# Selective scan of a Mamba block: two states in one scan instruction, the products with C in place over the states

## The reference, cut to what matters

```python
dt = jax.nn.softplus(dt_r @ W_dt + b_dt)
A = -jnp.exp(A_log)
h = 0                                             # [batch, 512 channels, 16 states]
for t in range(512):                              # lax.scan over the tokens
    dA = jnp.exp(dt[t][..., None] * A)            # "decay"
    h = dA * h + dt[t][..., None] * B[t][:, None, :] * x[t][..., None]     # the last term: "drive"
    y[t] = jnp.einsum('bds,bs->bd', h, C[t])
y = y + xc * D
y = y * jax.nn.silu(z)
attn = y @ W_out
P = x @ U1;  H = gelu(P @ V1 + b1);  Q = H @ U2;  ffn = Q @ V2 + b2        # beside it, used as a gate
```

## Time and profile before

| | us |
|---|---|
| time, median of 3 runs | 4176.64 (4173.5 to 4176.8) |
| span of the profiled execution | 4176.4 |
| scan stage in it, from the first drive to the last store | 304 to 1181, 877 long |
| busy in the stage: DVE / POOL / PE / ACT | 832.7 / 790.8 / 761.2 / 573.1 |

### The profile page before, as it was taken

How to read it: one execution, slowest core, us unless ns; L and a number is a source line. 1 busy time by engine, 2 the same in 40 slices (tenths; PEclk the granted TensorE clock), 3 DMA queues, 4 the chain that set the end, 5 groups by cost and what they waited for, 6 DMA issues and landing times. The chain is left out here.

```text
span 4176.4 us, 58564 instructions
## 1 busy us (share of the span) xinstructions
PE 3436.1 (82%) x17002; PEld 1831.7 (44%) x17002; DVE 3225.2 (77%) x5162; ACT 2286.7 (55%) x2729; POOL 1675.2 (40%) x783
## 2 busy tenths in 40 slices
PE   6847898889979978759799995699986977787775
PEld 3412333333347756635344442599975541222112
DVE  6869999999978877637687785487775768888884
ACT  4756666666622335424366663122212648989995
POOL 0008998989931100022000000000024338889986
PEclk9878999999989989968799998899998987888887
DMA  3453333333223357538423231211113452334332
GB/s 105 162 194 138 126 129 117 130 128 132 96 81 117 120 135 180 131 101 275 109 72 75 65 80 34 91 43 48 40 56 113 146 155 89 120 109 122 118 111 66
DMA packets 294113, 465.41 MB, mean 111 GB/s; under 512 B 40439, under 2 KB 237688, under 8 KB 273518
## 3 DMA queue, kind: packets, MB, share of 16 engines
q1 hardware_dynamic: 243590, 406.11, 30.0%
q10 hardware_dynamic: 50408, 57.97, 5.2%
HBM read 322.44 MB, written 141.33 MB: 111 GB/s over the span
## 5 line engine op out<-in xcount | busy, mean ns | idle before, releaser
L3314 POOL TENSOR_TENSOR distance_dist<-distance_dist,distance_least_all 128x2048 f32<-128x2048 f32 x128 | 577.0, 4537 | 113.5 <-DMA distance_least_all<-distance_least_rows 101.5
L1044 PE MATMUL mamba_psum<-mamba_hc,mamba_ident 128*128 128x512 f32 x1024 | 544.8, 643 | 86.7 <-DVE mamba_hc L947 69.9
L886 POOL TENSOR_TENSOR mamba_drive<-mamba_u,mamba_b_all 128x1024 f32<-128x1024 f32 x256 | 597.7, 2352 | 21.6 <-DMA mamba_b_all<-bc 21.6
L934 ACT ACTIVATE mamba_psum<-mamba_dt,mamba_a_neg 128x512 f32<-128x512 f32 x512 | 334.6, 683 | 288.7 <-DVE mamba_hc L947 281.6
L969 DVE TENSOR_TENSOR_SCAN mamba_psum<-mamba_psum,mamba_drive 128x512 f32<-128x512 f32 x352 | 414.9, 1215 | 43.7 <-POOL mamba_drive L886 29.4
L2355 DVE TENSOR_REDUCE causal_row_max<-causal_psum 128x1 f32<-128x512 f32 x512 | 332.7, 683 | 113.1 <-PE causal_psum L2411 103.0
L1044 PEld LDWEIGHTS mamba_psum<-mamba_hc,mamba_ident 128*128 128x128 f32 x1024 | 176.3, 195 | 410.6 <-DVE mamba_hc L947 223.5
L2314 ACT ACTIVATE causal_probs<-causal_psum 128x1024 f32<-128x1024 f32 x256 | 252.4, 1022 | 118.2 <-PE causal_psum L2434 116.0
L3407 DVE TENSOR_REDUCE distance_least<-distance_psum 128x2 f32<-128x1024 f32 x256 | 294.5, 1214 | 14.6 <-PE distance_psum L3466 14.1
L3425 DVE TENSOR_SCALAR distance_dist<-distance_psum 128x1024 f32<-128x1024 f32 x192 | 227.1, 1220 | 99.4 <-PE distance_psum L3481 93.4
L3466 PE MATMUL distance_psum<-distance_shared_k_stacks,distance_shared_q_stacks 102*128 102x512 bf16 x512 | 206.2, 499 | 118.1 <-DVE distance_least L3407 56.4
(11 more groups left out here) (455 smaller groups left out, 8228.5 us busy)
## 6 DMA issues: line engine op xcount, KB each, us to landing
mamba_b_all<-bc SPq DMA_DIRECT2D x32, 1024.0 KB
mamba_c_all<-bc SPq DMA_DIRECT2D x32, 1024.0 KB, 6.6
distance_least_all<-distance_least_rows SPq DMA_DIRECT2D x32, 1024.0 KB, 4.6
expert_weights_w<-L_ffn_w SPq DMA_DIRECT2D x16, 1024.0 KB, 4.8
z<-mamba_in_z SPq DMA_DIRECT2D x8, 1024.0 KB
xc<-mamba_in_xc SPq DMA_DIRECT2D x8, 1024.0 KB, 3.9
dt<-mamba_in_dt SPq DMA_DIRECT2D x8, 1024.0 KB, 3.9
u<-mamba_in_u SPq DMA_DIRECT2D x8, 1024.0 KB, 4.2
```

The lines of the kernel that those rows point to most:

```text
L886: pool.tensor_tensor(drive[:, n % DRIVES:n % DRIVES + 2], u[:, slot, m].unsqueeze(1).broadcast_to([P, 2, T]), b_all[:, s:s + 2], ALU.mult) ...
L934: act.activation(ps[:, DECAY_BANK + n % RING], dt[:, slot, m], ACT.Exp, scale=a_neg[:, m, s:s + 1]).then_inc(decay_ready, 1)
L1044: pe.matmul(ps[:, Y_BANK + m % 2], ident[:, :], hc[:, n % PRODUCTS], start=False, stop=(s == DS - 1)).then_inc(y_summed, 1)
L3314: pool.tensor_tensor(dist[:, g % 2, kt], dist[:, g % 2, kt], least_all[:, g % 2], ALU.subtract).then_inc(shifted, 1)
```

## The change

Two states (a pair `p`) are scanned in one instruction over 1024 elements. The decays of a pair lie in two neighbouring PSUM banks, of which two pairs exist; the decay of token 0 is never written by ACT and stays 0.0 from a memset at the stage's start, so that the state does not run over from the first state's last token into the second's first. The scan always writes to SBUF, `h`, a ring of 4 pairs. The products with C are made in place over `h`, on DVE for 11 of 16 states (`ON_DVE`: per 8 pairs, three instructions of one state and four of two) and on POOL for 5 (`ON_POOL`: three of one state and one of two). The drives are made four states at a time, in a ring of two such chunks. `hc` is gone. ACT's exponentials of pair p wait for the scan of pair p-2; the scan of pair p waits until PE has summed pair p-4.

```diff
-RING = 4
+PAIRS = STEPS // 2
 CHUNK = 4
-DRIVES, PRODUCTS = 8, 8
-POOL_STATES = (2, 5, 8, 11, 14)
+DRIVES, STATES = 2, 4
+ON_POOL = {0: slice(0, 1), 2: slice(0, 1), 4: slice(0, 1), 6: slice(0, 2)}
+ON_DVE = {0: slice(1, 2), 1: slice(0, 2), 2: slice(1, 2), 3: slice(0, 2), 4: slice(1, 2), 5: slice(0, 2), 7: slice(0, 2)}
...
-        drive = c.sb("drive", [P, DRIVES, T])
-        h = c.sb("h", [P, 2, T])
-        hc = c.sb("hc", [P, PRODUCTS, T])
+        drive = c.sb("drive", [P, DRIVES, CHUNK, T])
+        h = c.sb("h", [P, STATES, 2, T])
...
+        def decays(p):
+            return ps[:, DECAY_BANK + p % 2 * 2:DECAY_BANK + p % 2 * 2 + 2]
+        def state(p, part):
+            return h[:, p % STATES, part]
+        def c_rows(p, part):
+            first = p * 2 % DS
+            return c_all[:, first + part.start:first + part.stop]
...
 GpSimd
+                def times_c(p, b):
+                    part = ON_POOL[p % (DS // 2)]
+                    pool.wait_ge(h_ready, b * PAIRS + p + 1)
+                    if p < DS // 2:
+                        pool.wait_ge(c_loaded[p * 2 // CHUNK], b * DMA + DMA)
+                    pool.tensor_tensor(state(p, part), state(p, part), c_rows(p, part), ALU.mult).then_inc(hc_pool_ready, 1)
...
                 def scan(n, b, slot):
+                    if n % CHUNK:
+                        return
-                    if n % 2 == 0:
-                        wait_past(pool, h_ready, b * STEPS + n + 2 - DRIVES)
-                        pool.tensor_tensor(drive[:, n % DRIVES:n % DRIVES + 2], u[:, slot, m].unsqueeze(1).broadcast_to([P, 2, T]),
-                                           b_all[:, s:s + 2], ALU.mult).then_inc(drive_ready, 1)
-                    if n >= 3 and on_pool(n - 3):
-                        times_c(n - 3, b)
+                    wait_past(pool, h_ready, b * PAIRS + (n + CHUNK - DRIVES * CHUNK) // 2)
+                    pool.tensor_tensor(drive[:, n // CHUNK % DRIVES], u[:, slot, m].unsqueeze(1).broadcast_to([P, CHUNK, T]),
+                                       b_all[:, s:s + CHUNK], ALU.mult).then_inc(drive_ready, 1)
+                    if n:
+                        times_c((n - CHUNK) // 2, b)
+                    if n == STEPS - CHUNK:
+                        times_c(n // 2, b)
...
 ScalarE
+                act.wait_ge(starts_made, 1)
...
-                    if n >= RING:
-                        if on_pool(n - RING):
-                            act.wait_ge(h_ready, b * STEPS + n - RING + 1)
-                        else:
-                            act.wait_ge(hc_ready, b * DVE_HC + dve_products(n - RING))
...
-                    act.activation(ps[:, DECAY_BANK + n % RING], dt[:, slot, m], ACT.Exp, scale=a_neg[:, m, s:s + 1]).then_inc(decay_ready, 1)
+                    if not second:
+                        wait_past(act, h_ready, b * PAIRS + p - 1)
+                    act.activation(decays(p)[:, second, 1:], dt[:, slot, m, 1:], ACT.Exp,
+                                   scale=a_neg[:, m, s:s + 1]).then_inc(decay_ready, 1)
...
 VectorE
+                dve.memset(ps[:, DECAY_BANK:DECAY_BANK + 4, 0:1], 0.0).then_inc(starts_made, 1)
+                dve.wait_ge(starts_made, 1)
...
-                    dve.tensor_tensor(hc[:, n % PRODUCTS], ps[:, DECAY_BANK + n % RING], c_all[:, n % DS], ALU.mult).then_inc(hc_ready, 1)
+                    dve.tensor_tensor(state(p, part), state(p, part), c_rows(p, part), ALU.mult).then_inc(hc_ready, 1)
...
-                    if m >= 1 and s == 5:
+                    if m >= 1 and s == 6:
                         gated(b, slot, m - 1)
-                    dve.wait_ge(decay_ready, b * STEPS + n + 1)
...
-                    dve.tensor_tensor_scan(out, bank, drive[:, n % DRIVES], 0.0, ALU.mult, ALU.add).then_inc(h_ready, 1)
-                    if n >= 1 and not on_pool(n - 1):
-                        times_c(n - 1, b)
+                    dve.wait_ge(decay_ready, b * STEPS + n + 2)
+                    dve.wait_ge(drive_ready, b * NCHUNK * MT + n // CHUNK + 1)
+                    wait_past(dve, y_summed, b * STEPS + n + 2 - 2 * STATES)
+                    flat = "p s t -> p (s t)"
+                    dve.tensor_tensor_scan(state(p, slice(0, 2)).rearrange(flat), decays(p).rearrange(flat),
+                                           drive[:, n // CHUNK % DRIVES, n % CHUNK:n % CHUNK + 2].rearrange(flat),
+                                           0.0, ALU.mult, ALU.add).then_inc(h_ready, 1)
+                    if p >= 1 and (p - 1) % (DS // 2) in ON_DVE:
+                        times_c(p - 1, b)
+                    if p == PAIRS - 1:
+                        times_c(p, b)
...
 TensorE
-                    pe.matmul(ps[:, Y_BANK + m % 2], ident[:, :], hc[:, n % PRODUCTS], start=False, stop=(s == DS - 1)).then_inc(y_summed, 1)
+                    if n % 2:
+                        return
+                    p = n // 2
+                    for table, ready, count in ((ON_DVE, hc_ready, DVE_HC), (ON_POOL, hc_pool_ready, POOL_HC)):
+                        part = table.get(p % (DS // 2), slice(0, 0))
+                        for k in range(part.start, part.stop):
+                            if k == part.start:
+                                pe.wait_ge(ready, b * count + products(table, p))
+                            pe.matmul(ps[:, Y_BANK + m % 2], ident[:, :], h[:, p % STATES, k], start=False,
+                                      stop=(s + k == DS - 1)).then_inc(y_summed, 1)
```

More of the change, by code:

```diff
@@ L734, in nothing, with products @@
     pass
[L737 to L750, removed]
+def products(table, p):
+    m, pair = divmod(p, DS // 2)
+    return m * len(table) + sum(k <= pair for k in table)
 def stage_mamba_scan(nc, w, x_in, xc_in, z_in, dt_in, u_in, bc_in, low_in, x_out):
@@ L881, in scan @@
                         pool.wait_ge(du_loaded[slot], loads_before(b, slot) + 2 * DMA)
-                    if m == 0 and s % CHUNK == 0:
+                    if m == 0:
                         pool.wait_ge(b_loaded[s // CHUNK], b * DMA + DMA)
-                    if n % 2 == 0:
-                        wait_past(pool, h_ready, b * STEPS + n + 2 - DRIVES)
-                        pool.tensor_tensor(drive[:, n % DRIVES:n % DRIVES + 2], u[:, slot, m].unsqueeze(1).broadcast_to([P, 2, T]),
-                                           b_all[:, s:s + 2], ALU.mult).then_inc(drive_ready, 1)
-                    if n >= 3 and on_pool(n - 3):
-                        times_c(n - 3, b)
-                    if n == STEPS - 1:
-                        for last in (n - 2, n - 1, n):
-                            if on_pool(last):
-                                times_c(last, b)
+                    wait_past(pool, h_ready, b * PAIRS + (n + CHUNK - DRIVES * CHUNK) // 2)
[5 more added lines that the diff above has]
+                        times_c(n // 2, b)
                 beside_scan(pool, scan, nothing, nothing, nothing)
@@ L923, in scan @@
                     m, s = divmod(n, DS)
+                    p, second = divmod(n, 2)
                     if n == 0:
                         act.wait_ge(du_loaded[slot], loads_before(b, slot) + 2 * DMA)
[L926 to L934 removed]
+                    if not second:
+                        wait_past(act, h_ready, b * PAIRS + p - 1)
+                    act.activation(decays(p)[:, second, 1:], dt[:, slot, m, 1:], ACT.Exp,
+                                   scale=a_neg[:, m, s:s + 1]).then_inc(decay_ready, 1)
                 beside_scan(act, scan, ffn, nothing, nothing)
@@ L957, in scan @@
                     m, s = divmod(n, DS)
-                    if m >= 1 and s == 5:
+                    p, second = divmod(n, 2)
+                    if second:
+                        return
+                    if m >= 1 and s == 6:
                         gated(b, slot, m - 1)
-                    dve.wait_ge(decay_ready, b * STEPS + n + 1)
-                    dve.wait_ge(drive_ready, b * (STEPS // 2) + n // 2 + 1)
-                    bank = ps[:, DECAY_BANK + n % RING]
-                    if on_pool(n):
-                        k = pool_products(n) - 1
-                        wait_past(dve, hc_pool_ready, b * POOL_HC + k - 1)
-                        out = h[:, k % 2]
-                    else:
-                        out = bank
-                    dve.tensor_tensor_scan(out, bank, drive[:, n % DRIVES], 0.0, ALU.mult, ALU.add).then_inc(h_ready, 1)
-                    if n >= 1 and not on_pool(n - 1):
-                        times_c(n - 1, b)
-                    if n == STEPS - 1 and not on_pool(n):
-                        times_c(n, b)
+                    dve.wait_ge(decay_ready, b * STEPS + n + 2)
[9 more added lines that the diff above has]
+                        times_c(p, b)
                 def finish(n, b, slot):
```

28 lines of the change are left out of this document (7 added, 21 removed).

## The result

The changed kernel takes 4536.32 us (median of 4 runs, 4532.4 to 4543.5) against 4175.07 before: 1.0868 times as long, 95% interval 1.0852 to 1.0884. The way was forecast (slower, +270 us), the size was not: +361 us, above the range's end of 4520. Span of the profiled execution: 4536.6 us.

A forecast was written before the change was run, and what follows sets the result against it. DVE was taken as the bound, POOL 42 us behind. Stage: cycles 1067 + 38 multiplications + 6 `skip_diag` + 4.5 first drives + 12 end + 19 late decays = 1146, 270 above 877: 4446 us, range 4280 to 4520.

The forecast's parts named there:

- The exclusion: In the stage, DVE instructions with two SBUF inputs and POOL instructions reading SBUF exclude each other for their whole length.
- the cycle: Per chunk of four states: DVE product 0.61, drives 4.50, DVE product 1.14, scan 2.20, together 8.45 us against 6.85; chance 0.70.
- s + 2.81 to s + 6.25: Span of DVE's two-state product, waiting included, counted from s, the end of the last chunk's second pair scan.
- 1 to 3 us: Sign to look for: mean duration of DVE's two-state product, far above 1.23 us, ending just behind the drives' end.
- scan B: DVE's scan of the second pair in a chunk of four states, 2.20 us, behind the first pair's two-state product.
- The stage without late decays: The changed stage with the excluding instructions but no wait for decays behind Gelus: 1127 us.
- the 822: The changed stage without any coupling: DVE's own 806 us, 4.5 for the first drive, 12 at the end; 55 less.
- 64 x 0.3 = 19 us: Decays late behind Gelus: ready at s + 6.5, wanted at s + 6.25 by each chunk's second scan, 64 times.
- the case of the forecast: A Gelu whose `hid` follows two sums on PE, ending near s + 3.8; decays come at s + 6.5, wanted s + 6.25.
- The port-free rival: DVE products and POOL don't exclude each other, decays come late: stage 986 us, +109, kernel 4285; chance 0.06.
- the 163: Late decays when DVE products need not wait for POOL: 2.55 us late, 64 times, 163 us.
- Packing: Rival: DVE products and POOL's work alternate without idling, stage 995 us, +118, kernel 4294; 0.11 from this to 4390.

The follow-up runs named there:

- both_later: The changed kernel with the Gelu moved one step, between two pairs, and the Silu moved to step 2 of the next batch: 4418.06 us.
- gelu_later: The changed kernel with only the Gelu moved one step, between two pairs instead of between a pair's two exponentials: 4460.08 us.
- one_input: The changed kernel with DVE's products replaced by a maximum over the same elements, reading one SBUF tensor; leaves out products with C for 11 of 16 states: 4387.62 us.
- small_both_later: The changed kernel with drives of two states again, in the same ring of eight states, and with Gelu and Silu moved: 4325.87 us.

## Why the prediction was wrong, by its own steps

**The exclusion** was right in mechanism and direction, and nearly in the cycle. DVE's two-state product waits for the drives' end and goes first there. Its 3.40 us are what the cycle implied (from s + 2.81 to s + 6.25), while the "1 to 3 us" among the signs to look for was written carelessly, and the one-state product, which the same passage had far above 0.69, met a free port, as the cycle had it (0.66). The cycle is 8.23 us, not 8.45: the drives start 0.16 us behind the start of the one-state product, take 4.86 and so end 5.02 us behind it, where I had 0.61 + 4.50 = 5.11, and scan B starts 1.01 us behind their end, where I had 1.14. The stage without late decays was forecast at 1127 us and is 1111 (`both_later`). Taking the second SBUF input away, with the decays in time, gives 225 us (4418 to 4193). The forecast's own figure for this, 1127 - 822 = 305, was too large, and the 822 was too small: the version with neither cause has a stage of 884 us and is 20 us above the kernel before, not 55 below. The two errors nearly cancel in the sum (1127 against 1111), which was luck. Of the 62 us between 822 and 884, some 25 are DVE's waits for the very first drives and the end of the stage (25.4 us in two waits, and 15.6 from the last scan to the last store, in the changed kernel, where I had 4.5 and 12), and the size of the drives is 6 in the traces (884 to 878) or 11 in the times; the rest is steps and waits that no run took apart.

**The step that failed is "64 x 0.3 = 19 us"**, the decays. It measured 76 us for the Gelus by `gelu_later` (67 us as waits), and another 48 us for the Silu, which no term had. 118 instead of 19 us are 99 too few, and the prediction was 90 too low (4446 against 4536). In the trace of the changed kernel the chain behind a Gelu is the one I wrote down, but I took it at its best. Timeline of PE, DVE and ACT around two Gelus of one batch:

```profile
697.55 3.78 PE L1048 MATMUL mamba_psum<-mamba_h,mamba_ident 128*128 128x512 f32 x4 [3.77 <-DVE mamba_h L947]
701.12 1.87 PE L1039 MATMUL mamba_psum<-mamba_xc,mamba_skip_diag 128*128 128x512 f32 x2
702.83 1.88 PE L1048 MATMUL mamba_psum<-mamba_h,mamba_ident 128*128 128x512 f32 x4
704.64 1.12 PE L1015 MATMUL mamba_psum<-mamba_low,mamba_v 64*128 64x512 f32 x2
...
708.52 2.29 DVE L967 TENSOR_TENSOR_SCAN mamba_h<-mamba_psum,mamba_drive 128x1024 f32<-128x1024 f32 x1 [2.20 <-ACT mamba_psum L931]
717.25 2.29 DVE L967 TENSOR_TENSOR_SCAN mamba_h<-mamba_psum,mamba_drive 128x1024 f32<-128x1024 f32 x1 [0.40 <-ACT mamba_psum L931]
...
705.80 0.69 ACT L912 ACTIVATE mamba_hidden<-mamba_psum,mamba_b 128x512 f32<-128x512 f32 x1 [4.08 <-PE mamba_psum L1015]
714.53 0.69 ACT L912 ACTIVATE mamba_hidden<-mamba_psum,mamba_b 128x512 f32<-128x512 f32 x1 [1.69 <-PE mamba_psum L1015]
```

The Gelu at 714.53 is the case of the forecast, with a wait of 0.40 us. The one at 705.80 is not. Ahead of its `hid` lie the sums of the group before and the `skip_diag` multiplication that begins a group, and PE works at half speed: two states take 3.78 us instead of 1.98, the `skip_diag` 1.87 instead of the 1.02 it takes at full clock in the kernel before. The windows of 696 to 704 and 704 to 712 us give the clock (0.57 and 1.00):

```profile
696.00:704.00 8.00, 6.45 (x9) 2.76 (x10) 8.00 (x5) 3.75 (x5) 6.84 (x3) 0.57 0.00 0
704.00:712.00 8.00, 5.23 (x12) 1.47 (x11) 5.80 (x5) 5.01 (x7) 3.96 (x3) 1.00 0.00 0
```

Scan B waits 2.20. Over the run, 48 of the 64 Gelus make a scan wait: 16 by 0.4 us, about the 0.3 of the forecast, and 32 by 1.3 to 3.2. The other 16, for f = 3 and 7, make none. PE had been idle for 3.77 us, waiting for DVE's product, when it started at 697.55 at half speed. That the port's waiting pulls the clock down in this way is not shown: in `both_later` PE waits nearly as long for the same products and often goes on at full speed, as here:

```profile
588.52 1.98 PE L1050 MATMUL mamba_psum<-mamba_h,mamba_ident 128*128 128x512 f32 x4 [3.56 <-DVE mamba_h L949]
```

**The Silu** was left out because at the old kernel's lead of four states it costs nothing (no scan there waits more than 0.3 us for a decay), and I followed only the chain of the Gelu. The change shortens that lead to two pairs, one of which is being scanned; every operation in ACT's stream that waits for PE had to be walked through, not the most frequent one.

**The port-free rival** ("no exclusion, late decays", 4285) is nearly a run of its own: `one_input` gave 4388, with 224 us of late decays against the 163 in it. Both of its terms were too small, the decays and the 822.

**Packing** (4294): `small_both_later` at 4326 shows how near one comes with shorter drives. With drives of four and the decays in time, the stage is 1111 us and not 995 (`both_later`), as argued.

**The account**, from 4174 to 4536, with the causes taken away in this order: decays 118, exclusion 225, size of the drives 11, rest 8. In the other order the exclusion is 149 and the decays 194 (4388 to 4193); only the sum of the two does not depend on it.

By the Trainium skill, page SBUF — State Buffer, section Who interferes with whom, the second of two such instructions blocks fully until the first is done. The runs agree: the stretch of DVE's products follows the length of POOL's instruction (3.40 us with drives of 4.5 us, 1.45 with drives of 2.35) and is zero with one SBUF input (1.20 and 1.22). They do not agree to the last tenth: a product that waits ends 1.1 us behind the drives, and alone it takes 1.23, which leaves about 0.1 us (an estimate from these two) that the two instructions share.

## What to carry to other kernels

Moving a DVE operand from PSUM to SBUF can cost more than any instruction it saves: here a DVE instruction with two SBUF inputs and POOL's instructions, all of which read SBUF, took turns for nearly their whole length. Look for it where POOL is busy, and look at the length of POOL's instructions. When a ring is shortened, walk through every instruction of the producing engine that waits for a third one, and take its chain at the lower clock and behind the rarest item, not at its median. An experiment that removes one of two causes shows less than it cost (149 of 225 here) when the other takes its cover; remove both, then each.

## What the runs showed of the hardware

- A waiting instruction gets the port at the end of the other engine's, ahead of that engine's next one: in the timeline the product of B ends 1.1 us after the drives, and POOL's next product, started at the drives' end, is stretched by 1.0 us; the means over the run (3.40 and 2.20 us) say that this is the usual case here.
- The TensorE clock over the stage was 0.94 before, 0.85 after, and 0.94 again in `both_later`, where the stage is still 234 us longer than before. In the changed kernel stretches of 1.2 GHz lie between ones of 2.4, with sums at 1.9 us a state instead of 1.0. PE's time waiting for DVE's products before the sums is much the same in both (331.6 us in 149 waits, the longest 5.0, against 298.2 in 166, the longest 3.6), so it does not by itself tell where the clock falls. Why it fell was not tried.
- Drives of four states cost the kernel before 24 us although they save POOL work.
